# A clear of 400 columns between the scatters on Pool, a drain taken out, and three pieces of work moved

## The reference

```python
h = tok(x)                                             # [32, 121, 128]
h = h + attn(layernorm(h))                             # 8 heads, column bias from the edges
xf = layernorm(h).reshape(-1, 128)                     # 3872 rows
logits = xf @ Wr + br                                  # 8 experts, the largest wins; its softmax gate is 1
out = h + where(argmax(logits) == e, relu(xf @ W1[e] + b1[e]) @ W2[e] + b2[e], 0) summed over e
```

## Time and profile before

| what | value |
|---|---|
| median of three runs | 279.65 us |
| the profiled execution's own time | 280.29 us |
| its span from the first to the last instruction | 278.5 us |
| mean granted TensorE clock (share of full speed) | 0.941 |
| PE busy | 248.1 us, 89% of the span |
| DVE busy | 181.4 us, 65% |
| ACT busy | 164.5 us, 59% |
| POOL busy | 144.8 us, 52% |
| DMA engines, mean rate | 65 GB/s |

### The profile page before, as it was taken

How to read it: one execution, slowest core, us unless ns; L and a number is a source line. 1 busy time by engine, 2 the same in 40 slices (tenths; PEclk the granted TensorE clock), 3 DMA queues, 4 the chain that set the end, 5 groups by cost and what they waited for, 6 DMA issues and landing times.

```text
span 278.5 us, 8985 instructions
## 1 busy us (share of the span) xinstructions
PE 248.1 (89%) x2852; PEld 208.4 (75%) x2852; DVE 181.4 (65%) x679; ACT 164.5 (59%) x405; POOL 144.8 (52%) x275
## 2 busy tenths in 40 slices
PE   3999889999999999999998978986999359999693
PEld 3946667788887778778777746876989259999593
DVE  3996454687978778787789874764754035654452
ACT  3973355777667667657765654663566036775550
POOL 8001833245577676776767455365236723524444
PEclk9997999999999999999999995999799658999888
DMA  4110399000001110101101125312054233320000
GB/s 116 32 49 0 98 350 302 14 2 2 2 23 37 38 32 28 38 20 38 38 25 32 38 77 150 81 54 74 18 138 134 87 100 96 105 70 21 28 23 0
DMA packets 14462, 18.20 MB, mean 65 GB/s; under 512 B 3992, under 2 KB 10556, under 8 KB 14417
## 3 DMA queue, kind: packets, MB, share of 16 engines
q1 hardware_dynamic: 10976, 11.23, 14.1%
q0 software_dynamic: 3296, 6.00, 7.5%
q10 hardware_dynamic: 144, 0.41, 0.5%
HBM read 10.58 MB, written 7.54 MB: 65 GB/s over the span
## 4 chain that ended last, share of the span: by engine, by line
PE 66%; issue 11%; DVE 6%; POOL 6%; another core or an unknown queue 6%; ACT 2%; DMA 1%; ACTq 1%; POOLq 1%; DVEq 0%
PE psS L1247 9%; PE psB L1147 9%; PE psS L1163 6%; PE psB L1237 6%; PE psO L1290 5%; PE psS L1173 4%; PE psO L1237 4%; PE psB L1131 3%; POOL region_d L435 3%; DVE nmax L946 2%; PE psS L1143 2%; PE psO L1268 2%; PE psU L1280 2%; PE psB L1153 2%
## 5 line engine op out<-in xcount | busy, mean ns | idle before, releaser
L442 POOL DMA_INDIRECT out<-y_out,sidx x38 | 37.1, 977 | 46.0 <-DVE y_out L875 28.7
L946 DVE TENSOR_REDUCE nmax<-psS 121x8 f32<-121x968 f32 x32 | 37.2, 1163 | 15.3 <-PE psS L1173 14.0
L885 DVE TENSOR_SCALAR hT<-psS,b1T 128x128 f32<-128x128 f32 x76 | 23.2, 346 | 35.0 <-PE psS L1247 19.9
L1247 PE MATMUL psS<-xgT,W_tile 128*128 128x128 f32 x304 | 44.6, 295 | 0.8 <-ACT W_tile L558 0.6
L1247 PEld LDWEIGHTS psS<-xgT,W_tile 128*128 128x128 f32 x304 | 41.3, 211 | 1.7 <-ACT W_tile L558 1.4
L435 POOL DMA_INDIRECT region_d<-rows,pos x32 | 34.5, 1077 | 13.0 <-issue 11.2
L610 ACT ACTIVATE PT<-psS 121x968 f32<-121x968 f32 x32 | 31.3, 977 | 16.5 <-DVE nmax L946 14.2
L573 ACT ACTIVATE hT<-psS,b1T 128x128 f32<-128x128 f32 x76 | 23.8, 364 | 28.0 <-PE psS L1247 19.8
L1237 PE MATMUL psB<-W_sb,hT 128*128 x168 | 25.5, 300 | 7.1 <-ACT hT L573 6.0
L1237 PEld LDWEIGHTS psB<-W_sb,hT 128*128 128x128 f32 x168 | 22.8, 211 | 8.1 <-issue 8.1
L558 ACT ACTIVATE W_tile<-W_sb 128x512 f32 x38 | 23.9, 630 | 6.0 <-issue 4.4
(11 more groups left out here) (268 smaller groups left out, 543.5 us busy)
## 6 DMA issues: line engine op xcount, KB each, us to landing
xg<-region_d SPq DMA_DIRECT2D x38, 129.0 KB, 2.0
W_sb<-in_L_ffn_W SPq DMA_DIRECT2D x1, 2048.0 KB, 9.5
region_d<-pads SPq DMA_DIRECT2D x1, 1032.0 KB, 6.9
out<-y_out,sidx POOLq DMA_INDIRECT x38
b_bc<-in_L_ffn_b SPq DMA_DIRECT2D x1, 512.0 KB, 5.1
region_d<-rows,pos POOLq DMA_INDIRECT x32
xs<-in_x ACTq DMA_DIRECT2D x1, 402.5 KB, 3.7
edge_i<-in_L_attn_edge_index SPq DMA_DIRECT2D x1, 64.0 KB, 4.0
```

The lines of the kernel that those rows point to most:

```text
L442: pool.indirect_dma_start(out, bass.IndirectOffsetOnAxis(sidx[:, s:s + 1], 0), y_out[:, u, :], None, bounds_check=N - 1, oob_is_err=False) ...
L946: dve.tensor_reduce(nmax[0:L, :].rearrange("p (j c) -> p j c", c=HB)[:, :, HD + 1:HD + 3], score_half(0), AX.X, ALU.max, negate=True).then ...
L1247: ins = pe.matmul(psS[:, c // 2 * 2 + s % 2, c % 2 * 128:(c % 2 + 1) * 128], W1_tile[:, s % 2, c * 128:(c + 1) * 128], xgT[:, s % 2, :], s ...
```

## The change

- A tensor `pause` of 400 columns and a semaphore are added. `spare_clear` lets POOL write zeros into it; nothing reads it. A clear stands ahead of the scatters of the rows of the last five sequences and of the results of tiles 1 to 37, which makes 42 clears. From the second on, POOL first waits for the clear before.
- The result of tile 0 is scattered inside the last steps (step B+3), where the rows of sequence B-6 were scattered; those rows go out after the last norm.
- The waits of the first seven result scatters for later tiles are gone, and so is the drain.
- In steps B-2 and B-1 the rows of group five (sequences 20 to 23, two in a step) are scattered one ahead of the step's `rstd2` and one behind it; before, both stood together, ahead of it in step B-2 and behind it in step B-1.
- ACT reads the expert number of tile 0 ahead of the copy `turned_copy` of step B-1; before, it read it behind that copy, inside `W1_copy(0)`.

```diff
+        pause = sb("pause", [128, 400])
...
+            def spare_clear():
+                if pauses[0] > 0:
+                    pool.wait_ge(s_pause, pauses[0])
+                pool.memset(pause[:, :], 0.0).then_inc(s_pause, 1)
+                pauses[0] += 1
...
-                if has(t, 4) and t >= B - 1:
+                if t >= B - 2:
+                    scatter_rows(done)
                     rstd2(t - 4)
-                while done < B and scatter_step(done) <= t and done <= t - 8:
+                    scatter_rows(done + 1)
+                    done += 2
+                while t < B - 2 and done < B and scatter_step(done) <= t and done <= t - 8:
                     scatter_rows(done)
                     done += 1
...
-                if has(t, 4) and t < B - 1:
+                if has(t, 4) and t < B - 2:
                     rstd2(t - 4)
             for t in range(B, STEPS):
                 if t == B + 3:
-                    scatter_rows(B - 6)
-                    done = B - 5
+                    scatter_out(0)
...
-            for b in range(done, B):
+            scatter_rows(B - 6)
+            for b in range(B - 5, B):
+                spare_clear()
                 scatter_rows(b)
-            for s in range(NT):
-                if s < ALONG + 2:
-                    pool.wait_ge(f_y, s + 7)
+            for s in range(1, NT):
+                spare_clear()
                 scatter_out(s)
-                if s == NT - 14:
-                    pool.drain()
...
+                if t == B - 1:
+                    act.wait_ge(r_eid, 1)
+                    first_expert = expert_of(0)
                 if has(t, 4):
                     turned_copy(t - 4)
                 if t == B - 1:
-                    act.wait_ge(r_eid, 1)
                     act.wait_ge(l_ffn, 48)
-                    W1_copy(0)
+                    W1_copy(0, first_expert)
```

More of the change, by code:

```diff
@@ L227, in build @@
         f_b1, f_b1T, f_w1 = sem("f_b1"), sem("f_b1T"), sem("f_w1")
+        s_pause = sem("s_pause")
         N_CONST = 18
@@ L443, in scatter_out @@
                                         bounds_check=N - 1, oob_is_err=False).then_inc(f_sca[u], 16)
+            pauses = [0]
+            def spare_clear():
[3 more added lines that the diff above has]
+                pauses[0] += 1
             pool.wait_ge(s_rowid, 1)
@@ L475, in _ @@
                     scatter_rows(B - 7)
-                    done = B - 6
-            for b in range(done, B):
+            scatter_rows(B - 6)
+            for b in range(B - 5, B):
+                spare_clear()
                 scatter_rows(b)
-            for s in range(NT):
-                if s < ALONG + 2:
-                    pool.wait_ge(f_y, s + 7)
+            for s in range(1, NT):
+                spare_clear()
                 scatter_out(s)
-                if s == NT - 14:
-                    pool.drain()
         @block.scalar
@@ L552, in _, with expert_of, W1_copy @@
             tile_expert = [None, None]
-            def W1_copy(s):
-                e = act.value_load(eid[0:1, s:s + 1], min_val=0, max_val=E - 1)
+            def expert_of(s):
+                return act.value_load(eid[0:1, s:s + 1], min_val=0, max_val=E - 1)
+            def W1_copy(s, e=None):
+                if e is None:
+                    e = expert_of(s)
                 if s >= 2:
```

## The result

The changed kernel takes 266.88 us (median of four runs, 266.15 to 269.57) against 279.46 us for the kernel before beside it: a ratio of 0.9554 with an interval of [0.947, 0.9638], so **4.5% faster**. The forecast was 261 us, with a range of 257 to 275. The profiled execution took 266.91 us, with a span of 265.2. That is 13.4 us less than the profiled execution of before (280.29).

The account below looks back on a forecast made before the run. Late signals beside POOL's back-to-back scatters were taken to hold up the late expert tiles. POOL's limit of 258.1, 20.4 below the 278.5 span, gave 259.9; with no slack between two limits, 261 us was written, range 257 to 275.

Parts of the forecast that it names:

- The reading of the slices: TensorE's lower clock was placed late in the span, around slices 27 to 30 and 35, in the expert tiles' stage.
- The period: On POOL, a result scatter behind a clear every 1.69 us (0.97 + 0.30 + 0.42), between bounds of 1.62 and 1.90.
- the tiles' limit: Late expert tiles: first target number at 203.0, 26 steps of 1.90, result and scatter; the span ends at 258.0.
- The pair 1.67 apart: Two scatters at 199.06 and 200.73 that held nothing; taken as evidence that signals are not late at 1.69 us.
- The early pieces: Steps B-2 and B-1: 1.0 us from parting group five's rows, 0.5 from reading the expert's number earlier; together 1.5.
- 26 steps of tiles: The steps between the 27 late tiles would take 49.4 us at 1.90 each, in place of 66.0.
- rival 1: Late expert tiles: late signals become fewer but stay, 0.37 us a tile, tiles end 9.6 later; 269 us, chance 0.12.
- The closing part: From the last scatter's start to the end of the span: 2.86 us, as before the change.
- Rival 4: The removed drain's work is needed and falls on a scatter: 277 us, no difference; chance 0.10.
- Rival 2: In each late tile a clear holds one DVE instruction, 0.42 us each, 10.9 over 26 tiles: 271 us, chance 0.05.
- Rival 3: Waiting results, not scatter spacing, cause late signals; each scatter still costs 1.12 us while results wait: 271 us, chance 0.10.
- Rival 5: Late tiles from 194 on: queued clears keep every scatter costly, 1.12 us on each of 26 tiles; 289 us, chance 0.08.

Follow-up runs that it names:

- experiment 1: The changed kernel without its 42 clears; drain and waits stay out, moved pieces stay moved: 275.63 us, ratio 0.9814.
- experiment 2: The kernel before with the clears alone added; drain, waits and old order stay: 271.66 us, ratio 0.9671.
- experiment 5: The changed kernel with clears of 200 columns in place of 400: 273.35 us, ratio 0.9755.
- experiment 6: The changed kernel with clears of 560 columns in place of 400: 266.42 us, ratio 0.9491.
- experiment 4: The changed kernel with group five's rows and the read of the first expert's number put back where they were: 270.25 us, ratio 0.9631.
- experiment 3: The changed kernel with the drain put back after the result of tile 24: 268.01 us, ratio 0.9572.
- experiment 7: The changed kernel with drains behind the 4th, 12th, 20th and last scatter of rows: 267.17 us, ratio 0.9545.
- the kernel with three drains: The changed kernel with 480-column clears ahead of results and drains behind the 4th, 12th and 20th scatter of rows: 265.17 us, ratio 0.9584.

## Why the prediction was right, and where it was not

The direction, the place and the first mechanism were right: the holes went when the scatters were parted, and experiments 1, 2 and 5 show that the clears do it. The time was 5.9 us over the forecast of 261. Step by step:

- **The reading of the slices** was off, though not of the place: the low clock of the earlier trace rows stands in slices 25, 29, 32 to 34 and 38 to 40, not in 27 to 30 and 35. The holes from 214 us on lie in and just ahead of 32 to 34.
- **The period** was predicted at 1.69 and is 1.585 for results, 1.655 for rows, the first below even its lower bound of 1.62. The clear's length was sized well (0.45 against 0.42). What failed was the gap: a scatter behind a scatter waits 0.30, one behind a clear only 0.16. The sentence from the Trainium skill (Perfetto Trace Analysis, GPSIMD Engine Instruction), to time POOL from start to start, pointed to the better side; by the prediction's own sums its 1.62 takes off 0.1 us at most, not 0.2, since the tiles' limit stays at 258.0. With the nearer period came a cost: at 1.585 signals are still late, at 1.715 they are not (experiment 6). The pair 1.67 apart on which the forecast rested was a poor test: in experiment 2 the first of the long pieces in the chain begins at 211.89, just ahead of the third scatter of the train (211.97), and a pair ends before that.
- **The early pieces**: 1.5 predicted, 1.2 to 2.2 measured (experiment 4).
- **Last rows**: the fourth-last was predicted at 187.4 and the last at 192.6; they went at 187.12 (behind the second clear) and 192.09. **Result 1** was predicted at 194.35 and went at 193.73.
- **First late target number**: 203.0 predicted, 204.04 measured, 1.0 late.
- **26 steps of tiles**: 49.4 predicted, 51.0 measured. The 1.6 us are more than made up by the three slow steps between 205 and 214 us (together 3.1 us over 1.90 each). This is rival 1 in small: late signals stayed, but for one backlog at the start and not for all 26 tiles.
- **Result and its scatter**: 1.5 and 1.2 predicted, 1.5 and 1.5 measured.
- **The closing part is the step that failed.** It was taken over as 2.86 us, and "the drain costs nothing further, as POOL has scatters to send all the time" counted the removed 6.51 us as gone. It is 7.08 us. Experiments 3 and 7 and the kernel with three drains show that the drain takes longer, the more scatters have gone since the last one; taken out of the middle, it is owed at the end, where nothing covers it. That is 4.2 of the 7.0 us by which the sum (259.9) was short: 1.0 + 1.6 + 0.3 + 4.2, less 0.1 outside the span. Rival 4 had the drain come back, but on a scatter in the middle and for its whole length.
- **Rival 2** (DVE held up by clears) falls. The target numbers take 149 ns in the median (148 before). Few of them meet a clear: three in the changed kernel (150 to 159 ns) and ten with 560 columns (148 to 161); the longest of the 27, 210 ns, met none. The Trainium skill's SBUF — State Buffer (Who interferes with whom) has a VectorE instruction of two inputs contend with POOL instructions that read, not with those that only write; these times agree with it.
- **Rival 3** (backlog, not spacing) was half of the truth: without a backlog no long train forms, and in experiment 1, where waits and drain are gone too, the stretch from the last rows to the last target number fell from 80.4 to 70.7 us without a clear. Within a backlog it is the spacing that sets the price.
- **Rival 5** (the clear keeps each scatter costly) falls: with 560 columns, still with clears and a backlog, no step is slow.

**Left open.** Why other engines' signals wait for the scatters, no run shows; it goes neither by bytes nor by the rows of a result. Theory S2 had the order right, but its picture, a fixed 1.7 us for each scatter, is not shown: what is missing to 1.7 is 0.43 us at 1.275 apart and 0.12 at 1.585, and a scatter there cost 1.12 and 0.6. Whether plain idling of POOL would part the scatters as well as a clear does was not tried in a train; in the kernel before the scatters 1.90 apart, with idling between them, held nothing.

## What to carry to other kernels

When a profile shows work that is done but picked up microseconds later ("remote", "unknown queue"), look at what another engine issues back to back in that stretch, and try to part it before looking for a missing dependency. Part it by measured distance: too near leaves part of the cost, too far makes the issuing engine the bound. The label can be missing: at 1.65 apart no idling was called "remote", and still products were taken up 1.3 us late, so compare the end of the input with the start of the engine that reads it. And when a drain is taken out, ask where its work will be done instead: the end of this program drains too, and three drains put into the attention cost nothing.

## What the runs showed of the hardware that was not expected

- A POOL scatter by indirect DMA takes 0.97 us on its engine, but in this kernel trains of them were free of late signals only from about 1.7 us apart: 1.65 still gave slow tile steps, 1.715 none. An eighth of the bytes or half of the result rows changed the time by +0.1% and +0.4%, within the intervals.
- POOL's drain costs 0.08 to 0.09 us for each scatter since the drain before it (3.07 us for 37, 4.14 for 50, 5.88 for 70), but the shortest took 1.7 us behind 13 results and 2.3 behind four scatters of rows. It does not go by the size of the results: behind 57 scatters, 25 of them of results, it took 4.81 us with whole results, with an eighth of their bytes and with half of their rows.
- A clear of 400 columns takes 0.45 us, one of 560 takes 0.59, and the next scatter follows 0.16 us later, not 0.30 as behind a scatter.
